# Spectral filter and graph convolution on one core: who issues two late loads, and when ScalarE copies a group's sum

## What is computed

```python
x_spec = adj.T @ x                                   # pass 1
h = layernorm(x + adj @ (exp(-evals * t)[:, None] * x_spec))   # pass 2
deg = sum(adj + I, axis=1)
out = layernorm(h + tanh(((adj + I) / deg) @ (h @ W) + b))     # pass 3
```

## Time and profile before

| | |
|---|---|
| median of 3 runs | 627.07 us (626.67 to 628.39) |
| the profiled execution | 626.41 us |
| its span, from the first to the last instruction | 624.5 us |
| busy: PE, DVE, ACT, POOL | 586.1, 515.2, 400.6, 365.8 us |
| mean granted clock of TensorE | 0.98 |
| moved by DMA | 174.67 MB |

### The profile page before, as it was taken

One profiled execution on the slowest core, in us unless ns is written; L12 is line 12 of the kernel. 1 busy time (PEld: TensorE's weight loads), 2 busy tenths in 40 slices (PEclk: granted clock), 3 DMA queues, 4 the chain that ended last, 5 costly groups with the idle time before them and its releaser, 6 DMA issues.

```text
span 624.5 us, 8078 instructions
## 1 busy us (share of the span) xinstructions
PE 586.1 (94%) x2486; PEld 453.4 (73%) x2486; DVE 515.2 (82%) x605; ACT 400.6 (64%) x860; POOL 365.8 (59%) x210
## 2 busy tenths in 40 slices
PE   5999999999985799999999999999999979999993
PEld 5888888888874566667888888888888756656661
DVE  4899999999896999798889789597777586999992
ACT  4999999999975644545665646445454445544553
POOL 0000000000131988877999999779786879895972
PEclk9999999999998799999999999999999989999997
DMA  8999999999999899999996999387996299999201
GB/s 306 409 408 407 410 409 409 409 409 409 409 260 281 222 307 261 271 271 256 317 240 178 269 267 313 85 236 207 257 243 169 79 338 329 347 337 335 54 18 50
DMA packets 125065, 174.67 MB, mean 280 GB/s; under 512 B 6884, under 2 KB 105700, under 8 KB 125032
## 3 DMA queue, kind: packets, MB, share of 16 engines
q1 hardware_dynamic: 72608, 121.68, 59.5%
q10 hardware_dynamic: 52424, 52.58, 31.1%
HBM read 172.13 MB, written 2.11 MB: 279 GB/s over the span
## 4 chain that ended last, share of the span: by engine, by line
PE 78%; POOL 9%; DVE 5%; ACT 3%; issue 2%; ACTq 1%; DMA 1%; DVEq 0%
PE ps L785 13%; PE ps L787 13%; PE ps L786 13%; PE ps L761 9%; PE ps L762 9%; PE ps L763 9%; POOL lo L423 7%; PE ps L781 6%; DVE vt L616 3%; PE ps L850 1%; PE ps L853 1%; PE ps L746 1%; ACTq L336 1%; POOL rstd L415 1%; ACT hi L476 1%
## 5 line engine op out<-in xcount | busy, mean ns | idle before, releaser
L423 POOL TENSOR_TENSOR lo<-vt,hi 128x1024 fp32r<-128x1024 f32 x129 | 327.4, 2566 | 57.4 <-ACT hi L476 56.5
L616 DVE STREAM_TRANSPOSE vt<-raw 128x1024 f32<-128x1024 f32 x184 | 222.3, 1226 | 64.7 <-PE ps L787 54.4
L476 ACT ACTIVATE hi<-vt 128x1024 fp32r<-128x1024 f32 x163 | 169.8, 1061 | 110.3 <-DVE vt L616 91.8
L599 DVE TENSOR_TENSOR lo<-raw,hi 128x1024 fp32r<-128x1024 f32 x124 | 155.5, 1257 | 17.1 <-ACT hi L462 7.9
L462 ACT ACTIVATE hi<-raw 128x512 fp32r<-128x512 f32 x256 | 159.0, 624 | 5.4 <-PE ps L763 2.4
L404 POOL TENSOR_TENSOR lo<-raw,hi 128x1024 fp32r<-128x1024 f32 x4 | 10.7, 2674 | 177.0 <-ACT hi L462 177.0
L785 PE MATMUL ps<-hi,s_hi 128*128 128x512 f32 x232 | 99.0, 427 | 9.7 <-issue 5.2
L761 PE MATMUL ps<-hi,xg_hi 128*128 128x512 f32 x256 | 100.2, 392 | 2.4 <-DVE lo L599 1.8
L762 PE MATMUL ps<-lo,xg_hi 128*128 128x512 f32 x256 | 99.6, 389 | 0.0
L763 PE MATMUL ps<-hi,xg_lo 128*128 128x512 f32 x256 | 99.6, 389 | 0.0
L785 PE MATMUL ps<-hi,p_hi 128*128 128x512 f32 x206 | 89.1, 433 | 5.4 <-POOL lo L423 5.4
(11 more groups left out here) (66 smaller groups left out, 515.9 us busy)
## 6 DMA issues: line engine op xcount, KB each, us to landing
raw<-in_adj_dram SPq DMA_DIRECT2D x63, 1024.0 KB, 14.7
raw<-in_adj_dram SPq DMA_DIRECT2D x90, 512.0 KB, 9.4
raw<-in_adj_dram ACTq DMA_DIRECT2D x88, 512.0 KB, 11.5
late_raw<-in_adj_dram SPq DMA_DIRECT2D x8, 512.0 KB, 11.3
late_raw<-in_adj_dram ACTq DMA_DIRECT2D x8, 512.0 KB, 13.5
xn<-in_x_dram SPq DMA_DIRECT2D x8, 256.0 KB, 14.4
x_sb<-in_x_dram SPq DMA_DIRECT2D x8, 256.0 KB, 13.3
out_dram<-x_sb ACTq DMA_DIRECT2D x7, 256.0 KB, 3.1
```

The source lines that it names most:

```text
L423: nc.gpsimd.tensor_tensor(lo[:, slot(p), :], vt[:, slot(p), :], hi[:, slot(p), :].bitcast(f32), ALU.subtract).then_inc(pool_lo_ready, 1)
L476: nc.scalar.activation(hi[:, slot(s), :], vt[:, slot(s), :], ACT.Copy).then_inc(hi_ready, 1)
L599: nc.vector.tensor_tensor(lo[:, q % RING1, :], raw[:, k, 2 * h:2 * h + 2, :].rearrange("p r n -> p (r n)"), hi[:, q % RING1, :].bitcast(f3 ...
L616: nc.vector.transpose(vt[:, slot(s), :].rearrange("p (m a i) -> p m a i", m=2, a=RB), load_buffer(st.load).rearrange("p (a m e i) -> p e m ...
```

## The change

ACT's block for loads 36 and 37 goes, and SP issues all four quarters of these two loads, at their place in its list. And ACT copies each group's sum (`ending2`) at since 1 instead of since 0: one position later, after the high part of that position. PE's transposes stay at since 1.

```diff
@@ sync
                 wait_buffer(sp, n)
-                load_quarters(sp, n, (0, 1))
+
+                load_quarters(sp, n, range(QN) if LOADS[n].buf >= BUFS and BEFORE[n] is None else (0, 1))
@@ scalar
             def ending2(g, since):
-                if since == 0:
+                if since == 1:
                     act.wait_ge(mm_done, END2[g] + 1)
                     nc.scalar.activation(stage[:, 0, :], acc2(g), ACT.Copy).then_inc(acc_out, 1)
@@ scalar, end of the loop over positions
                 for row in range(NG):
                     ending3(row, since3(p, row))
-                if p == END2[LAST] + LAG + 1:
-                    for n in range(NL):
-                        if LOADS[n].buf >= BUFS and BEFORE[n] is None:
-                            wait_buffer(act, n)
-                            load_quarters(act, n, (2, 3))
```

## The result

The changed kernel took 628.77 us (median of 20 runs, 627.07 to 639.03), the kernel before, over 20 runs beside them, 625.55 (624.17 to 628.39). The ratio is 1.0047, interval 1.0036 to 1.0058: **slower by 0.5%, some 2.9 us**, where 2.2 us faster was forecast. The ratio leaves out the execution at 639.03, which is over 1.5% longer than the fastest of the same kernel. The profiled execution took 628.88 us, its span is 627.1 (before 624.5), the mean granted clock 0.978.

The account below looks back on a forecast made before the run. PE was taken as the bound nearly everywhere (78% of the span). -3.8 us at group 7 and +1.6 in group 1 sum to -2.2, from 627.07 to 624.9 us; the 8-in-10 range is 622.9 to 628.2.

Parts of the forecast that it names:

- Part two, group 1: Before step 40: with the copy later, POOL's low part 36 precedes DVE's 35; +1.6 us, bounds 0 and 2.0.
- The other copies at nothing: Groups other than 1: the copy one position later is still ahead of PE or keeps its time; 0 us.
- Part one's gain at group 7: Steps 138 to 142: without ACT's four issues POOL's 4.23 us idle goes; -3.8 us, bounds 0 and -4.6.
- The clock: Rival: behind PE's idle before steps 40 and 142 the clock drops, 1.6 us each; 626.5 or 628.1 us; chance 0.27.
- Their landing must stay covered ... Cost 0: Loads 36 and 37 on SP: at 339 GB/s load 37 is complete by 522.5, in time; cost 0.
- ACT's later stalls at 0: ACT's issue stalls, such as at 532 and 559, shrink but gain PE nothing; 0, bounds -0.6 and +0.6 us.
- a queue on its own is slow: Rival: SP alone carries load 37, late above 3.24 us a quarter; 628.8 us at 3.8, 631.6 at 4.2; chance 0.07.

Follow-up runs that it names:

- the five other executions of the table: Profiled executions of loads_only, act_later, act_138_141, change_but_group1 and act_one_quarter, set beside the kernel before by when each low part ends.
- loads_only: The changed kernel with the copy left at since 0, so only the loads' issues move to SP; 627.19 us, ratio 1.0019 to the kernel before.
- the first run: Transfers alone, nothing computed: seven stages of eight transfers on SP or both queues; 205 to 207 GB/s in one half, 339 in different halves, 386 over all partitions.
- the three executions named above: Profiled executions in which SP alone carries loads 36 and 37: loads_only, the changed kernel and change_but_group1; load 37 complete at 533.2, 536.4 and 537.2.
- act_138_141: The kernel before, with ACT's issues for loads 36 and 37 split, one load each at positions 138 and 141; 622.65 us, ratio 0.9960.
- act_later: The kernel before, with ACT's issues for loads 36 and 37 split, one load each at positions 141 and 144; 629.84 us, ratio 1.0060.
- the runs of transfers by themselves: Two runs of seven stages, nothing computed: the first run, and one with other quarter pairs, orders and sizes, where quarters 2 with 3 had 200 GB/s.
- act_one_quarter: act_138_141 with SP issuing three quarters of loads 36 and 37 each and ACT only quarter 3; 624.35 us, ratio 0.9984 to the kernel before.
- change_but_group1: The changed kernel with only group 1's sum copied at since 0 as before; 628.25 us, ratio 1.0038 to the kernel before.

## Why the prediction was wrong, point by point

- **Part two, group 1: right.** Forecast +1.6, measured +1.55 (-0.14 to +1.41), by the mechanism named: low part 35 took 2.75 (2.8 said), PE waited 2.16 (2.2 said).
- **The other copies at nothing: right.** The offset stays at +1.4 from step 40 to 133.
- **Part one's gain at group 7: right.** Forecast -3.8, measured -3.6 here and -3.6 to -3.7 in the five other executions of the table without ACT's block ahead of high part 138. With group 1's 1.6 my times give low part 142 at 512.0 and it started at 512.00; POOL's idle for the variances was 1.45 (1.4 said).
- **The clock: the rival's size was right, but it is no term of the sum here.** It was given 1.6 us for a drop. Behind PE's 2.44 us of waiting the changed kernel lost 1.6 (low part 142 ended at -2.2, PE's product of step 143 at -0.6; the low parts show 1.2 of it by step 150), loads_only the same behind 2.46. Behind the 2.16 in group 1 nothing was lost. But with load 37 late the 1.6 doesn't reach the end: of the runs of loads_only, the six with a mean clock of 0.979 to 0.982 took 625.2 to 627.2 us and the six with 0.984 to 0.986 took 627.2 to 628.9.
- **The failed step: "Their landing must stay covered ... Cost 0".** It took the 339 GB/s of both queues for what two queues move together however the quarters lie on them, let at most four of ACT's quarters overtake (five did), and had load 37 complete by 522.5. It was complete at 536.4. The runs show that the 339 was two halves of the partitions at 170 each, SP in the lower and ACT in the upper, and that one half has 206, by one queue or by both (written or, untested, read: see the first run). With the quarters 2 and 3 of the late loads on SP, both queues want the upper half. From the landing of quarter 1 of load 36 at 510.7, nine quarters of the upper half had to pass until load 37 was complete (four of SP's, and ACT's of loads 38, 39 and the first of 40): 9 x 0.524 MB / 206 GB/s = 22.9 us gives 533.6, and 536.1 with a tenth, since ACT's second quarter of load 40 is partly ahead too.
- **The cost of the halved rate: +4.0 instead of 0**, by two ways that the trace shows side by side. PE waited 2.12 for a copy that stood behind ACT's 6.23 us of issues, then ran at half clock (0.61 in 538 to 541): by the ends of steps 153 and 154 these are all of the 3.9 that PE lost. And POOL got the low part of step 157 late, so that its low parts run 3.0 us behind those of before from 158 on; at step 162 PE waits for one of them again (0.51 us, as the 0.60 of the earlier trace rows). The two don't add up, since PE was as late as the low parts by then. The second way alone would have cost about as much: PE needs the low part of step 160, and in the three executions named above it stands at the 0.2 to 3.9 that the landing gives. The first alone wasn't tried. One thing stays unexplained: quarter 1 of load 37 (lower half) and quarter 3 of load 39 (upper) landed at 527.9 and 528.6, some 2 us later than two halves allow.
- **ACT's later stalls at 0, since "ACT's queue is shorter": wrong, and this was the way by which PE lost first.** It carries fewer quarters, but each waits longer: 2.98 and 6.23 us at the issues of loads 41 and 42, 0.92 and 2.30 before.
- **The rival "a queue on its own is slow"**, with a chance of 0.07, had the right consequence and about the right price (load 37 late at over 3.24 us a quarter; at 4.0 its working gives some 630, 3 over the 627.07 that it starts from, and 628.77 was measured beside 625.55) with the wrong mechanism: two queues moved no more than one where both were in one half. That its price fits is luck in part, as it has neither ACT's stall nor the clock. What spoke for the halves was in the kernel before, in the assignment of quarters 0 and 1 to SP and 2 and 3 to ACT. I read it as a way to share issues and not as a way to share partitions.

## What to carry to other kernels

When a transfer is moved from one queue to another, look at which partitions it writes, not only at the bytes that each queue carries: with this kernel's quarters two queues moved some 340 GB/s while one was in partitions 0 to 63 and the other in 64 to 127, and 206 while both were in one half. Relieve an engine of a block of issues by moving it a step later and splitting it (act_138_141, 0.4% faster than the kernel before), and check where the next issues of that queue will stall: three steps further on (act_later) the same edit was 0.6% slower. The mean GB/s of a stretch is a measurement of an arrangement, and holds only as long as that arrangement stands.

## What the hardware showed that had not been expected

- The DMA share doesn't tell a stretch that is held back: in the runs of transfers by themselves it was 1.11 to 1.13 at 200 to 207 GB/s and 1.00 at 386. The GB/s do.
- An issue stalled once four to five quarters of its own queue were in flight, and ended at about the time when one of them had landed: in the first stage of the first run of transfers the sixth, seventh and eighth issue ended at 5.43, 7.80 and 10.22, the first three landings were at 5.35, 7.81 and 10.30. So a lower rate makes the engine's stall longer: 2.30 us for load 42's two issues in the kernel before, 6.23 here. The eight transfers of 4 KB packets went out in 4.3 us with no stall, so the number of transfers isn't what counts.
- Behind PE's wait of 2.42 to 2.46 us before step 142 the clock fell to 1.2 GHz in the changed kernel, loads_only and act_later, and did not in act_138_141, act_one_quarter and change_but_group1. In the changed kernel it fell behind 2.12 us at 538 and not behind 2.16 at 280, and in change_but_group1 it stayed up behind 3.20 us (1.00 in 537.5 to 541.5). So the length of the wait alone doesn't decide; what does no run here shows.
- The profiled executions differ by up to 2.7 us at step 30, before the change does anything. A comparison of two spans alone would have put a part of that down to the edits; the offsets step by step do not.
